# Scores and skip of one more batch as plain fp32 products, in a cross-attention and feed-forward kernel on one core

## The chip, the core and the metric

The kernel runs on one core of a Trainium2 chip. Its time is the device time of one execution in microseconds (us); lower is better. A core has five engines with a queue each: TensorE (PE in the profile; its weight loads are PEld), VectorE (DVE), ScalarE (ACT), GpSimd (POOL) and the sync engine (SP), which here only starts transfers. Each engine works off its own instructions in order; semaphores tie the queues together.

## What is computed

For each of 32 batches, x is 128 rows of 1024 and ctx is 128 rows of 256:

```
xl = layernorm(x)                                  # over the 1024
q = Wq xl;  k = Wk ctx;  v = Wv ctx                # 128 channels
att = softmax(q^T k / sqrt(128))                   # 1024 x 256
x1 = x + Wskip xl + v att^T
out = x1 + layernorm(x1) @ dequant(qweight, scales, zeros) + bias    # 1024 x 1024
```

The weights of the last product are four-bit numbers, unpacked once. The products are wanted nearly in fp32 precision.

## The kernel before

Wq is folded into the keys, so the scores are a product of the centred rows of x (128 x 1024) with scaled keys (128 x 256): eight tiles of 128 x 256 for each batch, in four chunks of two tiles. The two tiles of a chunk lie in ps_e[j % 2], so chunk j can only be written when the exps of chunk j - 2 (of the batch before, for j below 2) have been read.

There are two ways to form scores and skip. Batches from WHOLE (4) on are *split*: centred rows, keys and skip weights are each held as a high part in fp32r and a low part (the difference), and a product is three fp32r matmuls, high-high, high-low and low-high (`HI_LO`, L974 for the scores, L1009 for the skip). Batches 0 to 3 are *whole*: centred rows, keys and skip weights stay in plain fp32 (x_whole, k_whole, wsk_whole, with one slot for each of the four) and a product is one fp32 matmul instruction of the program, which the trace records as two passes (L970, L1005). The low parts cost VectorE and GpSimd work, the high part of the rows a copy on ScalarE.

The work is a software pipeline. Each engine has a hand-written run_in for the first batches and a step(t) for t = 3 on; in step t the engines work on scores and softmax of batch b = t, on projections of batch n = t + 1, on the attention product, skip and second norm of a = t - 1, and on the feed-forward product of q = t - 2. What an engine does in a step, and in which order, stands in that list. The parts that matter here:
- TensorE, step (L1105): scores(b, 0), keys_values(n) (L978), skip(a, 0) (L1000) and attend(a, 0) (L1011), scores(b, 1), scores(b, 2), skip(a, 1), attend(a, 1), scores(b, 3), then 34 feed-forward matmuls (L1020, L1026).
- ScalarE, step (L582): centre(n) (L456), exps(b, 0) (L499), keys_hi(n) (L469), values_hi(n) (L481), centred_hi(n) (L463), exps(b, 1), exps(b, 2), probs_hi(b, 0) (L510, the fp16 high part of the probabilities, L515), exps(b, 3), context_hi, apply_norm2(a) (L519), probs_hi(b, 1), xn_high(a).
- VectorE, step (L869): a row maximum (L695) ahead of each exps and a reciprocal (L700, called invert) behind it, keys_lo(n) (L681) and values_lo(n) (L687) in the middle, residual(a, h) (L711), the statistics of the norms, aggregate2(a) (L725) with the variance (L731), probs_lo (L704), scale_product (L734), context_lo (L659).
- GpSimd, step (L413): normalise(b, 0) (L270), inverse_std1, centred_lo(n, 0) (L284), normalise(b, 1), normalise(b, 2), centred_lo(n, 1), inverse_std2(a) (L291, with the bias of the second norm in L297), normalise(b, 3), write_out(q, 0) (L262, the add into o_sb in L267), split_row_sum(a), xn_low(a), write_out of the other half.
- The sync engine loads x and ctx, turns the probabilities and the normed rows by DMA and stores the output.

The projected keys are split too, from batch 5 on (SPLIT_KEYS); context_lo at t = 3 makes the low part of batch 5's context for keys_values(5) (L988), which step 4 of TensorE needs. In the rows, a line such as L974 is a line of the kernel.

Of the kernel before, what the change touches and what calls it, by code (L numbers as in the profile page):

```python
# [11 lines left out]
ACT = mybir.ActivationFunctionType  # L12
# [3 lines left out]
def xattn_ffn_program(nc, x, ctx_in, wq, wk, wv, wskip, qweight, scales, zeros, bias, out):  # L16


    B, C, N = x.shape
    M = ctx_in.shape[2]  # L20
# [2 lines left out]
    HALF = 512  # L23
    SPLIT_KEYS = 5
    QUARTER = 256
    WHOLE = 4
    HALVES = N // HALF
    NT = N // P
    MT = M // P
# [16 lines left out]
    with es:  # L46
        def sb(name, shape, dt=F32):
            return es.enter_context(nc.sbuf_tensor("sb_" + name, shape, dt))
# [37 lines left out]
        k_hi, k_lo = (sb(n, [P, 2, M], F32R) for n in ("k_hi", "k_lo"))  # L86
        v_hi, v_lo = (sb(n, [P, 3, M], F16) for n in ("v_hi", "v_lo"))
        wsk_hi, wsk_lo = (sb(n, [C, 3, C], F32R) for n in ("wsk_hi", "wsk_lo"))
        x_whole, k_whole, wsk_whole = (sb(n, [P, WHOLE, k]) for n, k in (("x_whole", N), ("k_whole", M), ("wsk_whole", C)))
        prob = sb("prob", [P, 2, CHUNKS, TPC, M])  # L90
        neg_max = sb("neg_max", [P, CHUNKS, TPC])
        esum = sb("esum", [P, CHUNKS, TPC])
# [46 lines left out]
        def ran(b, back=0):  # L139
            return 0 <= b - back < B  # L140
# [106 lines left out]
        def _(pool):  # L247
# [165 lines left out]
            def step(t):  # L413
                m, n, b, a, q, c = t + 2, t + 1, t, t - 1, t - 2, t - 3
                if 0 <= c < B - 1:
                    write_out(c, 1)
                if ran(b):
                    normalise(b, 0)
                if ran(m):
                    inverse_std1(m)  # L420
                if ran(n):
                    centred_lo(n, 0)
                if ran(b):
                    normalise(b, 1)
                    normalise(b, 2)
                if ran(n):
                    centred_lo(n, 1)
                if ran(a):
                    inverse_std2(a)
                if ran(b):  # L430
                    normalise(b, 3)
                if ran(q) and a < B - 1:
                    write_out(q, 0)
                if ran(a):
                    split_row_sum(a)
                    xn_low(a)
                if ran(q) and a >= B - 1:
                    write_out(q, 0)
# [5 lines left out]
        def _(act):  # L444
# [11 lines left out]
            def centre(n):  # L456
                act.wait_ge(mv1_done, n + 1)
                if n > WHOLE:
                    act.wait_ge(xclo_done, HALVES * (n - WHOLE))
                act.activation(xc[:, :] if n >= WHOLE else x_whole[:, n, :], x_sb[:, n % 4, :],  # L460
                               ACT.Identity, bias=mv1[:, 0:1], scale=-1.0).then_inc(xc_done, 1)

            def centred_hi(n):  # L463
# [5 lines left out]
            def keys_hi(n):  # L469
                if n < 2:  # L470
                    act.wait_ge((k0_done, k1_done)[n], 1)
                else:
                    act.wait_ge(kv_done, n + 1)
                act.wait_ge(rstd1_done, n + 1)
                if ran(n, WHOLE + 2):
                    act.wait_ge(scores_done[3], n - 1)
                src = (ps_o[1], ps_y[0], ps_kv)[min(n, 2)]
                act.activation(k_hi[:, n % 2, :] if n >= WHOLE else k_whole[:, n, :], src[:, 0:M], ACT.Copy,
                               scale=rstd1[:, n % 2:n % 2 + 1]).then_inc(khi_done, 1)

            def values_hi(n):  # L481
                act.wait_ge(t_step, 4 * (n + 1))
                act.wait_ge(kv_done, n + 1)
                if ran(n, 3):
                    act.wait_ge(attn_done[1], n - 2)
                act.activation(wsk_hi[:, n % 3, :] if n >= WHOLE else wsk_whole[:, n, :], proj[:, SKIP, :], ACT.Copy, scale=sk_scale[:, :])
                act.activation(v_hi[:, n % 3, :], ps_kv[:, M:2 * M], ACT.Copy,
                               scale=v_scale[:, :]).then_inc(kvhi_done, 1)

# [92 lines left out]
            def step(t):  # L582
                n, b, a = t + 1, t, t - 1
                if ran(n):
                    centre(n)
                if ran(b):
                    exps(b, 0)
                if ran(n):
                    keys_hi(n)
                    values_hi(n)  # L590
                    centred_hi(n)
                if ran(b):
                    exps(b, 1)
                if ran(b):
                    exps(b, 2)
                    probs_hi(b, 0)
                if ran(b):
                    exps(b, 3)
                if ran(t + 2) and t >= 3:
                    if t == 3:  # L600
                        key_projection_hi()
                    context_hi(t + 2)
                if ran(a):
                    apply_norm2(a)
                if ran(b):
                    probs_hi(b, 1)
                if ran(a):
                    xn_high(a)
# [5 lines left out]
        def _(dve):  # L614
# [254 lines left out]
            def step(t):  # L869
                m, n, b, a, q, c = t + 2, t + 1, t, t - 1, t - 2, t - 3  # L870
                if ran(c) and c < B - 1:
                    scale_product(c, 1)
                if c == B - 1:
                    last_out(0)
                    last_out(1)
                if ran(b):
                    row_max(b, 0)
                if ran(n):
                    value_scale(n)
                if ran(m):  # L880
                    stats1(m, 0)
                    stats1(m, 1)
                    aggregate1(m)
                if ran(b):
                    invert(b, 0)
                if ran(m):
                    variance1(m)
                if ran(a):
                    residual(a, 0)
                if ran(b):  # L890
                    row_max(b, 1)
                    row_max(b, 2)
                if ran(a):
                    stats2(a, 0)
                if ran(b):
                    invert(b, 1)
                if ran(n):
                    keys_lo(n)
                    values_lo(n)
                if ran(b):  # L900
                    invert(b, 2)
                if ran(a):
                    residual(a, 1)
                if ran(b):
                    row_max(b, 3)
                if ran(a):
                    stats2(a, 1)
                    aggregate2(a)
                if ran(b):
                    invert(b, 3)  # L910
                    probs_lo(b, 0)
                if ran(m):
                    context_max(m)
                if ran(q):
                    scale_product(q, 0)
                if ran(m) and t >= 3:
                    if t == 3:
                        key_projection_lo()
                    context_lo(m)
                if a == B - 1:  # L920
                    last_low()
                if ran(b):
                    probs_lo(b, 1)
# [5 lines left out]
        def _(pe):  # L929
# [23 lines left out]
            def scores(b, j):  # L953
                if b < WHOLE:
                    if j == 0:
                        pe.wait_ge(xc_done, b + 1)
                        pe.wait_ge(khi_done, b + 1)
                else:
                    if j == 0:
                        pe.wait_ge(klo_done, b - WHOLE + 1)  # L960
                    if j % (CHUNKS // HALVES) == 0:
                        pe.wait_ge(xclo_done, HALVES * (b - WHOLE) + 1 + j // (CHUNKS // HALVES))
                if j >= 2:
                    pe.wait_ge(exp_done[j - 2], b + 1)
                elif ran(b, 1):
                    pe.wait_ge(exp_done[j + 2], b)
                for t in range(TPC):
                    cols = slice((j * TPC + t) * P, (j * TPC + t + 1) * P)
                    if b < WHOLE:
                        last = pe.matmul(ps_e[j % 2][:, t, :], x_whole[:, b, cols],  # L970
                                         k_whole[:, b, :], start=True, stop=True)
                        continue
                    for i, (s, m) in enumerate(HI_LO):
                        last = pe.matmul(ps_e[j % 2][:, t, :], xc_p[s][:, b % 3, cols], k_p[m][:, b % 2, :],  # L974
                                         start=i == 0, stop=i == 2)
                last.then_inc(scores_done[j], 1)
# [23 lines left out]
            def skip(a, h):  # L1000
# [1 line left out]
                if ran(a, 1):  # L1002
                    pe.wait_ge(x1_done[h], a)
                if a < WHOLE:
                    pe.matmul(ps_o[h][:, :], wsk_whole[:, a, :], x_whole[:, a, cols],  # L1005
                              start=True, stop=False)
                    return
                for i, (s, m) in enumerate(HI_LO):
# [145 lines left out]
```

## Time and profile before

| | |
|---|---|
| median of 3 runs | 517.02 us (516.99 to 517.34) |
| the profiled execution's own time | 517.71 us |
| its span in the trace | 515.6 us |
| TensorE busy | 496.5 us (96%) |
| GpSimd busy | 467.1 us (91%) |
| VectorE busy | 435.3 us (84%) |
| ScalarE busy | 376.8 us (73%) |
| share of the chain of work that ended last, TensorE | 83% |
| the same, GpSimd | 8% |

Times in the trace count from the start of the span. The ends of matmuls are modelled and neighbours overlap: for the pace of TensorE one reads the distance between the starts, not the durations. The chain that ended last is followed back from the last instruction, at each step to what released it. "[x <-y]" at the end of a timeline row is idle time ahead of the instruction and who ended it. A share of the whole span says little about one step, so the prediction goes by steps.

### The profile page before, as it was taken

The page shows a single profiled execution, that of the slowest core. Times are in us where ns is not written, and L with a number is a line of the kernel's source. Part 1 is how long each engine was busy: PE and PEld are TensorE (multiplying, and loading weights), DVE is VectorE, ACT ScalarE, POOL GpSimd, SP SyncE. Part 2 cuts the span into 40 slices and gives each one's busy share as a digit, 9 for nine tenths or more (in the row PEclk, how much of TensorE's full clock was granted, in tenths as well). Part 3 has the DMA queues.
Part 4 walks back from the last instruction along what each step waited for, and adds up shares of the span by engine and source line. Part 5 has one row for each costly group of instructions (what it writes and reads, how often), then busy time and mean ns, then how long its engine had stood idle before and what let it go on. Part 6 is the DMA issues. An engine that isn't in the chain of part 4 may idle for free.

```text
span 515.6 us, 9359 instructions
## 1 busy us (share of the span) xinstructions
PE 496.5 (96%) x2672; PEld 299.4 (58%) x2672; DVE 435.3 (84%) x1001; ACT 376.8 (73%) x867; POOL 467.1 (91%) x711
## 2 busy tenths in 40 slices
PE   4888999999999999999999999999999999999987
PEld 3544456665666656566665566666556666565644
DVE  4989898888988888898888889888889888887752
ACT  4889778777787777778777777877777877777520
POOL 4786999999999999999999999999999999999763
PEclk9999999999999999999999999999999999999999
DMA  8774678778968987887878786787767687757653
GB/s 305 204 156 108 183 176 157 204 187 187 197 171 202 156 199 183 196 182 179 211 150 193 185 206 176 180 204 156 196 178 197 172 202 190 168 130 145 167 130 120
DMA packets 227203, 92.65 MB, mean 180 GB/s; under 512 B 209488, under 2 KB 214352, under 8 KB 227152
## 3 DMA queue, kind: packets, MB, share of 16 engines
q1 hardware_dynamic: 226432, 91.91, 73.9%
q8 instruction: 21, 0.34, 0.3%
q14 instruction: 30, 0.25, 0.2%
q10 hardware_dynamic: 720, 0.14, 0.2%
HBM read 23.87 MB, written 16.78 MB: 79 GB/s over the span
## 4 chain that ended last, share of the span: by engine, by line
PE 83%; POOL 8%; issue 3%; DVE 3%; ACT 2%; DMA 1%; POOLq 0%; ACTq 0%; SPq 0%
PE ps_y L1020 38%; PE ps_e L974 15%; PE ps_o L1015 13%; PE ps_o L1009 7%; PE ps_kv L992 2%; PE ps_y L1026 2%; PE ps_kv L988 2%; POOL sb_prob L273 2%; POOL sb_xn_lo L318 2%; PE ps_e L970 1%; POOL sb_o L267 1%; DMA sb_x<-in_x_dram 1%; ACT sb_prob L506 1%; POOL sb_rstd L281 1%; DVE sb_neg_max L697 1%
## 5 line engine op out<-in xcount | busy, mean ns | idle before, releaser
L1020 PE MATMUL ps_y<-sb_wf,sb_xnt_hi 128*128 128x512 f16 x496 | 188.3, 380 | 3.3 <-DMA sb_xnt_lo<-sb_xn_lo 3.3
L1020 PE MATMUL ps_y<-sb_wf,sb_xnt_lo 128*128 128x512 f16 x496 | 188.0, 379 | 0.0
L506 ACT ACTIVATE sb_prob<-ps_e,sb_neg_max 128x256 f32<-128x256 f32 x256 | 118.2, 470 | 51.5 <-DVE sb_neg_max L697 51.4
L273 POOL TENSOR_SCALAR sb_prob<-sb_prob,sb_rsum 128x256 f32<-128x256 f32 x256 | 122.5, 492 | 7.3 <-DVE sb_rsum L702 7.2
L706 DVE TENSOR_TENSOR sb_p_lo<-sb_prob,sb_p_hi 128x1024 f16<-128x1024 f32 x64 | 78.1, 1220 | 36.5 <-ACT sb_p_hi L515 36.4
L267 POOL TENSOR_TENSOR sb_o<-sb_prod,sb_x 128x512 f32<-128x512 f32 x63 | 84.9, 1348 | 5.8 <-DVE sb_prod L740 5.8
L697 DVE TENSOR_REDUCE sb_neg_max<-ps_e 128x2 f32<-128x512 f32 x128 | 85.0, 682 | 1.8 <-PE ps_e L970 1.4
L515 ACT ACTIVATE sb_p_hi<-sb_prob 128x1024 f16<-128x1024 f32 x64 | 67.4, 1053 | 23.3 <-issue 23.3
L1020 PEld LDWEIGHTS ps_y<-sb_wf,sb_xnt_hi 128*128 128x128 f16 x496 | 48.4, 98 | 61.0 <-DMA sb_xnt_lo<-sb_xn_lo 4.3
L1020 PEld LDWEIGHTS ps_y<-sb_wf,sb_xnt_lo 128*128 128x128 f16 x496 | 48.5, 98 | 54.8
L974 PE MATMUL ps_e<-sb_k_hi,sb_xc_hi 128*128 128x256 f32 x224 | 78.6, 351 | 0.1
L524 ACT ACTIVATE sb_xn<-sb_x,sb_nb,sb_rstd 128x1024 f32<-128x1024 f32 x32 | 43.3, 1353 | 42.4 <-POOL sb_nb L297 42.4
L318 POOL TENSOR_TENSOR sb_xn_lo<-sb_xn,sb_xn_hi 128x512 f16<-128x512 f32 x63 | 71.8, 1161 | 0.2
L288 POOL TENSOR_TENSOR sb_xc_lo<-sb_xc,sb_xc_hi 128x512 fp32r<-128x512 f32 x56 | 71.2, 1272 | 0.0
L974 PE MATMUL ps_e<-sb_k_lo,sb_xc_hi 128*128 128x256 f32 x224 | 63.1, 281 | 0.0
L974 PE MATMUL ps_e<-sb_k_hi,sb_xc_lo 128*128 128x256 f32 x224 | 62.8, 280 | 0.0
L740 DVE TENSOR_TENSOR sb_prod<-ps_y,sb_scale_row 128x512 f32<-128x512 f32 x63 | 42.9, 682 | 11.2 <-PE ps_y L1026 6.3
L506 ACT ACTIVATION_READ_ACCUMULATOR sb_prob<-ps_e,sb_neg_max 128x1 f32 x256 | 51.1, 199 | 0.0
L716 DVE SCALAR_TENSOR_TENSOR sb_x<-ps_o,sb_o_scale,sb_x 128x512 f32<-128x512 f32 x64 | 47.3, 739 | 2.9 <-PE ps_o L1015 2.8
L1015 PE MATMUL ps_o<-sb_pt_hi,sb_v_hi 128*128 128x512 f16 x128 | 49.1, 384 | 0.4 <-DMA sb_pt_lo<-sb_p_lo 0.4
L1015 PE MATMUL ps_o<-sb_pt_hi,sb_v_lo 128*128 128x512 f16 x128 | 48.5, 379 | 0.0
L1015 PE MATMUL ps_o<-sb_pt_lo,sb_v_hi 128*128 128x512 f16 x128 | 48.5, 379 | 0.0
(150 smaller groups left out, 976.0 us busy)
## 6 DMA issues: line engine op xcount, KB each, us to landing
sb_x<-in_x_dram SPq DMA_DIRECT2D x32, 512.0 KB, 3.9
out_dram<-sb_o SPq DMA_DIRECT2D x63, 256.0 KB, 2.4
sb_ctx<-in_ctx_dram SPq DMA_DIRECT2D x32, 128.0 KB, 2.7
sb_q<-in_L_ffn_qweight_dram SPq DMA_DIRECT2D x4, 512.0 KB, 7.5
sb_pt_hi<-sb_p_hi SPq DMA_TRANSPOSE x64, 3.0
sb_pt_lo<-sb_p_lo SPq DMA_TRANSPOSE x64, 2.9
sb_scale_row<-in_L_ffn_scales_dram SPq DMA_DIRECT2D x1, 512.0 KB, 9.6
sb_xnt_hi<-sb_xn_hi SPq DMA_TRANSPOSE x32, 2.8
```

What stands on the lines that cost most here:

```text
L267: pool.tensor_tensor(o_sb[:, c % 2, cols], prod[:, h, :], x1[:, c % 3, cols], ALU.add).then_inc(out_done[h], 1)
L273: last = pool.tensor_scalar(prob[:, b % 2, j, t, :], prob[:, b % 2, j, t, :], rsum[:, j, t:t + 1], P_SCALE, ALU.mult, ALU.mult)
L288: pool.tensor_tensor(xc_lo[:, n % 3, cols], xc[:, cols], xc_hi[:, n % 3, cols].bitcast(F32), ALU.subtract).then_inc(xclo_done, 1)
L318: last = pool.tensor_tensor(xn_lo[:, k:k + KT // 2, :], xn[:, k:k + KT // 2, :], xn_hi[:, k:k + KT // 2, :], ALU.subtract)
L506: done = act.activation(prob[:, b % 2, j, t, :], ps_e[j % 2][:, t, :], ACT.Exp, bias=neg_max[:, j, t:t + 1], accum_out=esum[:, j, t:t + 1])
L515: act.activation(p_hi[:, h, :, :].rearrange("n k (t m) -> n k t m", m=P), prob[:, b % 2, 2 * h:2 * h + 2, :, :].rearrange("n j t (k m) -> ...
L697: dve.tensor_reduce(neg_max[:, j, :], ps_e[j % 2][:, :, :], AX.X, ALU.max, negate=True).then_inc(max_done[j], 1)
L706: dve.tensor_tensor(p_lo[:, h, :, :].rearrange("n k (t m) -> n k t m", m=P), prob[:, b % 2, 2 * h:2 * h + 2, :, :].rearrange("n j t (k m) ...
L716: dve.scalar_tensor_tensor(x1[:, a % 3, cols], ps_o[h][:, :], o_scale[:, a % 3:a % 3 + 1], x_sb[:, a % 4, cols], ALU.mult, ALU.add).then_i ...
L974: last = pe.matmul(ps_e[j % 2][:, t, :], xc_p[s][:, b % 3, cols], k_p[m][:, b % 2, :], start=i == 0, stop=i == 2)
L1015: last = pe.matmul(ps_o[h][:, :], v_p[s][:, a % 3, k * P:(k + 1) * P], pt_p[m][:, h, k, :], start=False, stop=k == MT - 1 and i == 2)
L1020: pe.matmul(ps_y[h][:, :], xnt_p[s][:, q % 2, kt, :], wf[:, kt, h * HALF:(h + 1) * HALF], start=kt == 0 and s == 0, stop=False)
```

## The change

Batch 4 becomes a whole batch. WHOLE is 5, while the three fp32 tiles keep their four slots (SLOTS); batch 4 uses slot 0, which was batch 0's. ScalarE gets two waits ahead of writing it: centre(4) waits for batch 0's attention product (behind its skip), keys_hi(4) for batch 0's last scores. For batch 4 centred_hi, centred_lo (two halves), keys_lo and the low part of the skip weights (in values_lo) are left out; scores (eight tiles) and skip (two halves) are one fp32 matmul each in place of three fp32r ones. SPLIT_KEYS stays at 5.

```diff
-    WHOLE = 4
+    WHOLE, SLOTS = 5, 4
...
-        x_whole, k_whole, wsk_whole = (sb(n, [P, WHOLE, k]) for n, k in (("x_whole", N), ("k_whole", M), ("wsk_whole", C)))
+        x_whole, k_whole, wsk_whole = (sb(n, [P, SLOTS, k]) for n, k in (("x_whole", N), ("k_whole", M), ("wsk_whole", C)))
...
-                if ran(n):
+                if ran(n) and n >= WHOLE:
                     centred_lo(n, 0)
...
-                if ran(n):
+                if ran(n) and n >= WHOLE:
                     centred_lo(n, 1)
...
                 if n > WHOLE:
                     act.wait_ge(xclo_done, HALVES * (n - WHOLE))
-                act.activation(xc[:, :] if n >= WHOLE else x_whole[:, n, :], x_sb[:, n % 4, :],
+                if SLOTS <= n < WHOLE:
+                    act.wait_ge(attn_done[1], n - SLOTS + 1)
+                act.activation(xc[:, :] if n >= WHOLE else x_whole[:, n % SLOTS, :], x_sb[:, n % 4, :],
                                ACT.Identity, bias=mv1[:, 0:1], scale=-1.0).then_inc(xc_done, 1)
...
                 if ran(n, WHOLE + 2):
                     act.wait_ge(scores_done[3], n - 1)
+                elif SLOTS <= n < WHOLE:
+                    act.wait_ge(scores_done[3], n - SLOTS + 1)
                 src = (ps_o[1], ps_y[0], ps_kv)[min(n, 2)]
-                act.activation(k_hi[:, n % 2, :] if n >= WHOLE else k_whole[:, n, :], src[:, 0:M], ACT.Copy,
+                act.activation(k_hi[:, n % 2, :] if n >= WHOLE else k_whole[:, n % SLOTS, :], src[:, 0:M], ACT.Copy,
                                scale=rstd1[:, n % 2:n % 2 + 1]).then_inc(khi_done, 1)
...
-                act.activation(wsk_hi[:, n % 3, :] if n >= WHOLE else wsk_whole[:, n, :], proj[:, SKIP, :], ACT.Copy, scale=sk_scale[:, :])
+                act.activation(wsk_hi[:, n % 3, :] if n >= WHOLE else wsk_whole[:, n % SLOTS, :], proj[:, SKIP, :], ACT.Copy, scale=sk_scale[:, :])
...
                     keys_hi(n)
                     values_hi(n)
+                if ran(n) and n >= WHOLE:
                     centred_hi(n)
...
                 if ran(n):
-                    keys_lo(n)
+                    if n >= WHOLE:
+                        keys_lo(n)
                     values_lo(n)
...
                     if b < WHOLE:
-                        last = pe.matmul(ps_e[j % 2][:, t, :], x_whole[:, b, cols],
-                                         k_whole[:, b, :], start=True, stop=True)
+                        last = pe.matmul(ps_e[j % 2][:, t, :], x_whole[:, b % SLOTS, cols],
+                                         k_whole[:, b % SLOTS, :], start=True, stop=True)
                         continue
...
                 if a < WHOLE:
-                    pe.matmul(ps_o[h][:, :], wsk_whole[:, a, :], x_whole[:, a, cols],
+                    pe.matmul(ps_o[h][:, :], wsk_whole[:, a % SLOTS, :], x_whole[:, a % SLOTS, cols],
                               start=True, stop=False)
                     return
```

## Rows read from the trace of the kernel before

**Rows 1.** Chain of waits in order of time: start us, us, what; "x" counts instructions.
```profile
75.11 0.31 POOL sb_xc_lo L288
...
480.33 0.75 DVE sb_x L716
```
**Rows 2.** Windows of step 4 and step 5: busy us and count of each engine, granted clock.
```profile
67.40:83.44 16.04, 15.82 (x85) 9.01 (x83) 14.45 (x33) 12.73 (x30) 15.64 (x24) 1.00 0.77 185
83.44:98.58 15.14, 15.14 (x87) 9.27 (x85) 13.55 (x32) 11.84 (x28) 14.82 (x22) 1.00 0.82 186
```
**Rows 3.** Timeline of TensorE, steps 4 and 5: start us, busy us, line, tiles.
```profile
68.28 0.18 PE L983 MATMUL ps_m<-sb_amax,sb_ones 128*128 128x1 bf16 x1
68.57 0.36 PE L988 MATMUL ps_kv<-sb_ctx_lo,sb_key_hi 128*128 128x256 f32 x1
...
74.97 0.38 PE L1015 MATMUL ps_o<-sb_pt_hi,sb_v_lo 128*128 128x512 f16 x1
75.46 0.39 PE L974 MATMUL ps_e<-sb_k_hi,sb_xc_hi 128*128 128x256 f32 x1
...
76.28 0.39 PE L1020 MATMUL ps_y<-sb_wf,sb_xnt_hi 128*128 128x512 f16 x1
...
84.33 0.18 PE L983 MATMUL ps_m<-sb_amax,sb_ones 128*128 128x1 bf16 x1
84.37 0.36 PE L988 MATMUL ps_kv<-sb_ctx_lo,sb_key_hi 128*128 128x256 f32 x1
```
**Rows 4.** Timeline of ScalarE, steps 3 and 4.
```profile
56.61 1.07 ACT L467 ACTIVATE sb_xc_hi<-sb_xc 128x1024 fp32r<-128x1024 f32 x1
58.19 0.47 ACT L506 ACTIVATE sb_prob<-ps_e,sb_neg_max 128x256 f32<-128x256 f32 x1 [0.52 <-DVE sb_neg_max L697]
...
59.91 0.21 ACT L506 ACTIVATION_READ_ACCUMULATOR sb_prob<-ps_e,sb_neg_max 128x1 f32 x1
62.54 1.06 ACT L515 ACTIVATE sb_p_hi<-sb_prob 128x1024 f16<-128x1024 f32 x1 [2.41 <-issue]
...
75.20 0.20 ACT L506 ACTIVATION_READ_ACCUMULATOR sb_prob<-ps_e,sb_neg_max 128x1 f32 x1
```
**Rows 5.** Timeline of TensorE, step 3: plain fp32 scores and skip of whole batches.
```profile
49.76 1.03 PE L970 MATMUL ps_e<-sb_k_whole,sb_x_whole 128*128 128x256 f32 x4
50.62 0.17 PE L983 MATMUL ps_m<-sb_amax,sb_ones 128*128 128x1 bf16 x1
...
51.61 1.02 PE L1005 MATMUL ps_o<-sb_x_whole,sb_wsk_whole 128*128 128x512 f32 x2
```
**Rows 6.** Chain of waits: split scores and a split skip where TensorE never waits.
```profile
87.43 1.43 PE ps_e L974 x12
...
452.32 0.69 PE ps_o L1009 x3
```
**Rows 7.** Timeline of GpSimd, step 3.
```profile
60.28 1.27 POOL L288 TENSOR_TENSOR sb_xc_lo<-sb_xc,sb_xc_hi 128x512 fp32r<-128x512 f32 x1
...
65.20 0.75 POOL L297 TENSOR_SCALAR sb_nb<-sb_mv,sb_rstd 128x1 f32<-128x1 f32 x1
...
66.83 1.30 POOL L267 TENSOR_TENSOR sb_o<-sb_prod,sb_x 128x512 f32<-128x512 f32 x1
```
**Rows 8.** Timeline of VectorE, steps 3 and 4.
```profile
59.34 0.47 DVE L684 SCALAR_TENSOR_TENSOR sb_k_lo<-ps_kv,sb_rstd,sb_k_hi 128x256 fp32r<-128x256 f32 x1
...
60.40 0.15 DVE L702 RECIPROCAL sb_rsum<-sb_esum 128x2 f32<-128x2 f32 x1
...
62.68 0.15 DVE L731 TENSOR_SCALAR sb_ve<-sb_mv 128x1 f32<-128x1 f32 x1
...
66.92 1.51 DVE L661 TENSOR_TENSOR sb_ctx_lo<-sb_ctx,sb_ctx_hi 128x256 fp32r<-128x256 f32 x1
...
73.67 1.28 DVE L697 TENSOR_REDUCE sb_neg_max<-ps_e 128x2 f32<-128x512 f32 x2
...
81.53 0.46 DVE L661 TENSOR_TENSOR sb_ctx_lo<-sb_ctx,sb_ctx_hi 128x256 fp32r<-128x256 f32 x1
```

## The prediction, made before the changed kernel ran

> **What bounds the kernel now.** The page's busy times come first: TensorE is the busiest engine, GpSimd the next. Then the chain of waits in order of time. Up to 75.42 us its pieces in steps 3 and 4 are GpSimd's; then come the last scores of batch 4, and from there it stays on TensorE up to 480.33 us, where the tail of the last batches begins [rows 1]. The windows say how firmly: step 5, from 83.44 to 98.58 us, holds 15.14 us of TensorE work in 15.14 us, and the 25 steps behind it are as long; step 4 holds 15.82 us in 16.04 [rows 2]. So an instruction that TensorE gains in step 5 or later moves the end by its whole length, while step 4 has holes that can take some in. What matters for GpSimd's place in the chain is how long TensorE itself stood still. Its timeline shows two holes. From L983 to L988 it needs 68.57 - 68.28 = 0.29 us where step 5 needs 0.04: 0.25 us lost. The last scores of batch 4 start at 75.46 us, while the attention matmul that started at 74.97 has left the array free after its usual 0.215 us of issue, at 75.18: 0.28 us lost. Behind that stop the chunk needs 0.82 us, up to the first L1020 at 76.28, where an undisturbed one needs half of 1.43, 0.71: another 0.11 us [rows 3, 6]. Step 4 can give back 0.25 + 0.28 + 0.11 = **0.64 us** at most. The holes of step 3 are out of reach: the first instruction that goes, the copy to xc_hi, starts at 56.61 us, and ScalarE waits behind it for VectorE's row maximum until 58.19 anyway [rows 4], so the exps that TensorE waits for in step 3 end when they do now.
>
> **What TensorE gets.** Each score chunk of two tiles becomes four passes of plain fp32 instead of six of fp32r. Fewer instructions, yet the distance between issues decides. A plain chunk takes 50.62 - 49.76 = 0.86 us, and its last result comes 0.17 us after that (1.03 us in all) [rows 5]. Two split chunks take 1.43 us [rows 6]. Four chunks: 4 x 0.86 = 3.44 against 2 x 1.43 = 2.86, **+0.58 us**, all in step 4. The skip goes from three passes of 512 columns, 0.69 us [rows 6], to two, which stream as much as a chunk's four of 256 and show 1.02 us with the same 0.17 of drain, 0.85 [rows 5]: +0.16 for each half, **+0.32 us**, in step 5, where nothing absorbs it. Together +0.90 us.
>
> A rule speaks against this price. The Trainium skill, FP8 and Floating Point Precision, section TensorE Precision Notes, says that true fp32 takes four passes through the array. Counted against the three of the split, by that rule both terms would be a third of the old time, (2.86 + 1.38) / 3 = 1.41 us, as an estimate. The trace puts a plain tile at 0.43 us, not at 4/3 of 0.36 = 0.48, so I stay with the rows.
>
> **What the other engines lose.** ScalarE drops 1.07 us into an idle stretch (above): nothing by itself. GpSimd drops both halves of xc_lo, 1.27 us each [rows 7]. VectorE drops k_lo, 0.47 us, and wsk_lo behind it [rows 8]. What then comes earlier, followed through the queues:
> - VectorE's next reciprocal, at 60.40 us [rows 8], needs ScalarE's exps, which end at 59.91 + 0.21 = 60.12 [rows 4]. Only some 0.26 us of what was dropped is a lead; the variance for the second norm, at 62.68 to 62.83 [rows 8], ends near 62.57.
> - GpSimd starts normalise(3,1) near 60.3, in the place of L288 at 60.28 [rows 7]. ScalarE's p_hi, at 62.54 now because it needs that normalise, starts 1.3 us earlier [rows 4], and so do the exps behind it. The bias of the second norm, 65.20 now [rows 7], needs only the reciprocal square root before it, 0.64 us behind the variance: near 63.24, 1.96 earlier.
> - VectorE works without a pause from the reciprocal behind those exps on, so their 1.3 us carries. Context_lo of batch 5, 66.92 + 1.51 = 68.43 us now, ends near 67.1 [rows 8]. It is what TensorE waits for in the first hole: it comes there at 68.28 now and at 68.43 behind the longer scores [rows 3]. Closed, with 1.3 us to spare.
> - TensorE comes to the last scores of batch 4 at 75.18 + 3/4 of 0.58 - 0.25 = 75.37 us. The maxima that release them start at 73.67 now [rows 8] and could start at 72.4, but need scores(4,1). Those leave TensorE before a chunk, a skip half and an attention half (6 x 0.215): 75.37 - 0.86 - 0.85 - 1.29 = 72.37, and 0.17 later they are there, 72.54. The exps behind the maxima, which end at 75.20 + 0.20 = 75.40 now [rows 4], then end near 74.3. Closed, with 1.1 us to spare.
>
> Behind step 4 the three engines are ahead, TensorE is not. The sync engine's queue keeps its transfers, with those of p_hi, p_lo and xn earlier. The two new waits on ScalarE (centre for batch 0's attention, keys_hi for its scores) are on counts reached long before 52 us; the exps are queued behind them. They cost nothing as long as ScalarE's idle stretch covers them, some hundredths without it.
>
> **Sum.** +0.58 + 0.32 - 0.64 = **+0.26 us**. The profiled execution took 517.71 us, its span 515.6; the change would put it at 517.97. It stands 0.69 above the median of the runs, 517.02, to which the same difference applies: 517.3 us. The unknown is how much of the 0.64 comes back: none gives +0.90, all +0.26, and I take all, since both leads are above 1 us.
>
> **The rivals.** A measurement of this kernel can tell about 0.2%, 1.03 us, from no change.
> - *The holes stay, or move.* Context_lo took 1.51 us for its usual 0.46 [rows 8] beside GpSimd's 1.30 us add into o_sb [rows 7]; a stretch of that kind can fall on another VectorE instruction now. Against: it takes over 1.1 us on a queue that is 1.3 ahead. Price: +0.90, 517.9 us. The Trainium skill, SBUF — State Buffer, section Who interferes with whom, says that a VectorE instruction with two SBUF inputs and a GpSimd one that reads SBUF exclude each other, and that issue order decides; the trace agrees, with that 1.51.
> - *Slower beyond that.* Two such stretches, 2 x 1.05 us, between VectorE's maxima of scores(4,0) and scores(4,1) use up the slack of 1.1 and put 1.0 us in front of the last scores. The point from which it decides is 1.1 us of delay there; then +0.26 + 1.0 = 1.26, 518.3 us. Against: step 4 has one such stretch now, before those maxima.
> - *A plain pass costs a third more than the split.* If scores and skips cost four passes of split length among their split neighbours, +1.41 - 0.64 = +0.77, 517.8 us. Against: plain skips stand in step 4 already, between split scores. It is what the rule of four passes makes of the time.
> - *Faster: GpSimd paces this stage, as the chain says.* Then 75.46 comes 1.3 us earlier and carries all behind it: -1.3 + 0.15 (the last plain chunk) + 0.32 = -0.8, 516.2 us; with all 2.5 us of GpSimd's -2.0, 515.0 us. Against: TensorE has 0.64 us of holes to lose there, not more.
> - *The tail uses a lead kept from step 4.* Against: the 26 steps between are paced by TensorE, so a lead is spent in waiting.
> That the change doesn't do what it says I leave out: slot 0 of the three tiles is free by then, and writer and readers index it alike.
>
> **Chances.** Forecast 0.70; holes stay 0.11; four passes 0.05; slower beyond 0.05; faster 0.05, about half of it inside 0.2%; something no row shows 0.04. So faster by over 0.2% 0.04, within 0.2% 0.87, slower by over 0.2% 0.09. The range reaches below the forecast by about the scatter of the runs, 0.35 us, and a little of the faster case, above through the holes that stay: 516.8 to 518.1 us.
>
> **What would show it.** On TensorE: 16 plain passes for batch 4's scores, 0.215 us apart; L988 0.04 us behind L983; no idle time ahead of the last scores; the first L1020 behind them within 0.1 us of 76.28; skips of batch 4 at 0.85; steps of 15.14 us behind. On GpSimd: normalise(3,1) near 60.3, then idle time ahead of its next add into o_sb. On VectorE: context_lo ending near 67.1. I am wrong if idle time stands ahead of a TensorE group of step 4 (first two rivals), or if batch 5's scores start well ahead of now (GpSimd's).

## The result: slower by half a per cent, most of it in the tail

The changed kernel takes 519.53 us (median of 6 runs, 519.02 to 521.11), the kernel before 517.03 (6 runs, 516.92 to 517.34): a ratio of 1.0051, 95% interval 1.0040 to 1.0061. That is slower, and outside the predicted range of 516.8 to 518.1 us. The profiled execution took 519.8 us, its span is 517.7.

The first look goes to the steps that the change touches. The timeline of the changed kernel, steps 3 to 5 (start us, busy us, engine, line, tiles; in this kernel L976 is the plain scores, L989 and L994 are what L983 and L988 were, L1021 what L1015 was, L1026 what L1020 was; L519 writes p_hi, L702 the row maxima):

```profile
60.19 1.83 POOL L273 TENSOR_SCALAR sb_prob<-sb_prob,sb_rsum 128x256 f32<-128x256 f32 x4
61.20 1.06 ACT L519 ACTIVATE sb_p_hi<-sb_prob 128x1024 f16<-128x1024 f32 x1 [1.17 <-issue]
63.24 1.30 POOL L297 TENSOR_SCALAR sb_nb<-sb_mv,sb_rstd 128x1 f32<-128x1 f32 x1
65.54 1.52 DVE L666 TENSOR_TENSOR sb_ctx_lo<-sb_ctx,sb_ctx_hi 128x256 fp32r<-128x256 f32 x1
...
68.33 0.17 PE L989 MATMUL ps_m<-sb_amax,sb_ones 128*128 128x1 bf16 x1
68.36 0.36 PE L994 MATMUL ps_kv<-sb_ctx_lo,sb_key_hi 128*128 128x256 f32 x1
...
72.46 0.69 DVE L702 TENSOR_REDUCE sb_neg_max<-ps_e 128x2 f32<-128x512 f32 x1
73.33 0.69 DVE L702 TENSOR_REDUCE sb_neg_max<-ps_e 128x2 f32<-128x512 f32 x1 [0.17 <-PE ps_e L976]
...
75.06 0.38 PE L1021 MATMUL ps_o<-sb_pt_hi,sb_v_lo 128*128 128x512 f16 x1
75.28 1.03 PE L976 MATMUL ps_e<-sb_k_whole,sb_x_whole 128*128 128x256 f32 x4
76.14 0.38 PE L1026 MATMUL ps_y<-sb_wf,sb_xnt_hi 128*128 128x512 f16 x1
...
84.19 0.18 PE L989 MATMUL ps_m<-sb_amax,sb_ones 128*128 128x1 bf16 x1
```

Both holes of [rows 3] are closed: L994 follows L989 by 0.03 us (0.29 before), and the last scores of batch 4 start 0.22 us behind the attention matmul ahead of them, with no idle time named. The chunk costs 76.14 - 75.28 = 0.86 us, as a plain chunk does in [rows 5]. Context_lo ends at 67.06, where 67.1 was forecast (it took 1.52 us again, as before, and the lead covers that); the bias of the second norm, p_hi and normalise(3,1) stand about 0.1 us from their forecasts or nearer. The chain of waits, which had GpSimd's xc_lo at 75.11 us [rows 1], is TensorE's alone from 59.86 us on, through both steps.

The windows of steps 4 and 5 say the same. Windows of the changed kernel (busy us and count of PE, PEld, DVE, ACT, POOL; then granted clock, DMA share, GB/s):

```profile
67.43:83.29 15.86, 15.81 (x74) 8.98 (x75) 14.20 (x32) 12.36 (x29) 15.07 (x22) 1.00 0.72 177
83.29:98.75 15.46, 15.41 (x84) 9.06 (x83) 13.48 (x32) 11.68 (x28) 14.46 (x22) 1.00 0.88 182
```

To see where the time went, one instruction is followed from batch to batch: the matmul with the column of ones (L983 before, L989 after), which stands once in each batch's keys. Its starts, from the timelines of TensorE, and the end of the span:

| stretch, us | before | after | difference |
|---|---|---|---|
| start of the span to batch 4 | 50.62 | 50.52 | -0.10 |
| batch 4 to 6 (scores, holes) | 33.71 | 33.67 | -0.04 |
| batch 6 to 7 (skip of batch 4) | 15.14 | 15.46 | +0.32 |
| batch 7 to 31 | 363.46 | 363.41 | -0.05 |
| batch 31 to the end of the span | 52.70 | 54.67 | **+1.97** |

So the change cost 0.28 us where it was made, and 2 us more than 380 us later. The table adds up to 2.10 us, by which the two profiled executions differ (2.09); the medians lie 2.50 apart. For the other 0.4 us there are the starts of single executions, which scatter by more than that, and a lower clock in two of the six runs (under e2).

There the chain of waits names the place; it is the same chain in both kernels up to the last transfer. First the kernel before, then the one after (start us, us, what):

```profile
494.28 2.84 DMA sb_xnt_lo<-sb_xn_lo
497.12 0.05 issue
497.16 2.98 PE ps_y L1020 x13
```

```profile
494.36 4.87 DMA sb_xnt_lo<-sb_xn_lo
499.23 0.05 issue
499.28 2.76 PE ps_y L1026 x12
```

The transfer that turns the low part of the normed rows of batch 30 starts 0.08 us later and takes 2.03 us more. TensorE has nothing else left to do. Its idle time in the grouped lines of 494 to 502 us (line, operation, tiles, count, busy us and mean ns, idle before and who ended it), before and after:

```profile
L1020 PE MATMUL ps_y<-sb_wf,sb_xnt_hi 128*128 128x512 f16 x11 | 4.2, 380 | 1.4 <-DMA sb_xnt_lo<-sb_xn_lo 1.4
```

```profile
L1026 PE MATMUL ps_y<-sb_wf,sb_xnt_hi 128*128 128x512 f16 x7 | 2.7, 381 | 3.4 <-DMA sb_xnt_lo<-sb_xn_lo 3.4
```

Windows of one microsecond show a stop and not a slow transfer (columns as above). Before, then after:

```profile
495.00:496.00 1.00, 0.80 (x4) 0.19 (x2) 0.47 (x2) 0.00 (x0) 0.44 (x1) 1.00 0.65 148
496.00:497.00 1.00, 0.00 (x0) 0.00 (x0) 0.97 (x2) 0.00 (x0) 0.00 (x0) 1.00 0.98 248
497.00:498.00 1.00, 0.84 (x4) 0.41 (x5) 0.68 (x3) 0.00 (x0) 0.17 (x1) 1.00 1.07 412
```

```profile
495.00:496.00 1.00, 0.88 (x5) 0.20 (x2) 0.47 (x2) 0.00 (x0) 0.51 (x1) 1.00 0.71 148
496.00:497.00 1.00, 0.00 (x0) 0.00 (x0) 0.97 (x2) 0.00 (x0) 0.00 (x0) 1.00 2.43 23
497.00:498.00 1.00, 0.00 (x0) 0.00 (x0) 0.76 (x3) 0.00 (x0) 0.09 (x1) 1.00 0.06 6
```

From 496 to 498 us the DMA engines move 23 and 6 GB/s, where they moved 248 and 412. A packet is put down whole to the time at which it began, which is how the share comes above 1: these packets are in flight and don't end. The DMA view of 490 to 500 us says what is new. Queues and the two transfers behind which the others wait, before and after (queue, kind: packets, MB, share; then transfer, KB, us to landing):

```profile
q14 instruction: 1, 0.01, 0.3%
...
out_dram<-sb_o SPq DMA_DIRECT2D x2, 256.0 KB, 2.3
...
sb_xnt_lo<-sb_xn_lo SPq DMA_TRANSPOSE x1, 2.8
```

```profile
q8 instruction: 1, 0.02, 1.2%
...
out_dram<-sb_o SPq DMA_DIRECT2D x2, 256.0 KB, 3.5
...
sb_xnt_lo<-sb_xn_lo SPq DMA_TRANSPOSE x1, 4.9
```

Queue q8 fetches instructions, 16,384 bytes at a time, 21 times in either run. Its single packets, and the slow ones of the transposes, as the trace has them (queue, start us, ns, bytes):

```
before   q8   489.75   992  16384
after    q8   495.48  1900  16384
after    q1   496.01  2134    256      18 such packets, 496.01 to 496.15,
after    q1   496.15  2005    256      2005 to 2138 ns; their neighbours take 18
```

The fetch, which stood ahead of the transposes of the normed rows, stands on the one of xn_lo, and 18 of that transfer's packets, begun while it runs, take 2.1 us for their usual 18 ns. Such packets are no feature of the tail: in all eleven traces together 730 packets of 256 bytes took over 1.5 us, and 719 of them were in flight during a fetch on q8. The kernel before has 20 of them (131.21 to 131.35 us, 1.86 to 2.00 us), where TensorE waits for nothing.

Why the fetch moved is a count. 21 fetches of 256 instructions hold 5,376, and TensorE issues about that: 5,502 before, of which 2,672 are matmuls, as many weight loads, the rest nearly all waits. The change takes ten matmul passes, ten weight loads and one wait from its queue: 21 instructions. (The page's counts of weight loads are 2,672 before and 2,662 after; of the matmuls after, 32 records are missing.) That leads to theory A: **the position of TensorE's last instruction fetch, not batch 4, costs the 2 us**.

### The profile page after: what moved, and what is told of

Read it like the earlier page. It is cut to its first block, busy times and chain, and to the rows that moved or that the text cites. A ratio compares the mean times of both kernels' runs of the same rounds, so it can differ in the third digit from the quotient of the medians.

```text
span 517.7 us, 9299 instructions
## 1 busy us (share of the span) xinstructions
PE 495.2 (96%) x2630; PEld 299.0 (58%) x2662; DVE 434.7 (84%) x999; ACT 376.4 (73%) x866; POOL 465.0 (90%) x709
## 4 chain that ended last, share of the span: by engine, by line
PE 85%; POOL 5%; DVE 3%; issue 3%; DMA 2%; ACT 2%; POOLq 0%; ACTq 0%; SPq 0%
PE ps_y L1026 40%; PE ps_e L980 14%; PE ps_o L1021 14%; PE ps_o L1015 7%; PE ps_kv L994 2%; PE ps_kv L998 2%; PE ps_e L976 2%; POOL sb_prob L273 1%; PE ps_y L1032 1%; POOL sb_xn_lo L318 1%; DMA sb_xnt_lo<-sb_xn_lo 1%; DMA sb_x<-in_x_dram 1%; DVE sb_neg_max L702 1%; ACT sb_prob L510 1%; PE ps_o L1011 1%
## 5 line engine op out<-in xcount | busy, mean ns | idle before, releaser
L1026 PE MATMUL ps_y<-sb_wf,sb_xnt_hi 128*128 128x512 f16 x496 | 188.3, 380 | 6.8 <-DMA sb_xnt_lo<-sb_xn_lo 5.2
L1026 PE MATMUL ps_y<-sb_wf,sb_xnt_lo 128*128 128x512 f16 x496 | 188.0, 379 | 0.0
L702 DVE TENSOR_REDUCE sb_neg_max<-ps_e 128x2 f32<-128x512 f32 x128 | 85.2, 683 | 1.8 <-PE ps_e L976 1.4
L1026 PEld LDWEIGHTS ps_y<-sb_wf,sb_xnt_hi 128*128 128x128 f16 x496 | 48.4, 98 | 62.8 <-DMA sb_xnt_lo<-sb_xn_lo 6.2
L519 ACT ACTIVATE sb_p_hi<-sb_prob 128x1024 f16<-128x1024 f32 x64 | 67.3, 1052 | 20.6 <-issue 20.6
L1026 PEld LDWEIGHTS ps_y<-sb_wf,sb_xnt_lo 128*128 128x128 f16 x496 | 48.5, 98 | 54.9
L980 PE MATMUL ps_e<-sb_k_hi,sb_xc_hi 128*128 128x256 f32 x216 | 75.9, 351 | 0.0
L288 POOL TENSOR_TENSOR sb_xc_lo<-sb_xc,sb_xc_hi 128x512 fp32r<-128x512 f32 x54 | 68.7, 1272 | 0.0
L980 PE MATMUL ps_e<-sb_k_lo,sb_xc_hi 128*128 128x256 f32 x216 | 60.8, 281 | 0.0
L980 PE MATMUL ps_e<-sb_k_hi,sb_xc_lo 128*128 128x256 f32 x216 | 60.6, 281 | 0.0
L1021 PE MATMUL ps_o<-sb_pt_hi,sb_v_hi 128*128 128x512 f16 x128 | 49.1, 384 | 0.4 <-DMA sb_pt_lo<-sb_p_lo 0.4
L1021 PE MATMUL ps_o<-sb_pt_hi,sb_v_lo 128*128 128x512 f16 x128 | 48.5, 379 | 0.0
L1021 PE MATMUL ps_o<-sb_pt_lo,sb_v_hi 128*128 128x512 f16 x128 | 48.5, 379 | 0.0
```

Source lines behind the costliest of these rows:

```text
L288: pool.tensor_tensor(xc_lo[:, n % 3, cols], xc[:, cols], xc_hi[:, n % 3, cols].bitcast(F32), ALU.subtract).then_inc(xclo_done, 1)
L519: act.activation(p_hi[:, h, :, :].rearrange("n k (t m) -> n k t m", m=P), prob[:, b % 2, 2 * h:2 * h + 2, :, :].rearrange("n j t (k m) -> ...
L702: dve.tensor_reduce(neg_max[:, j, :], ps_e[j % 2][:, :, :], AX.X, ALU.max, negate=True).then_inc(max_done[j], 1)
L1021: last = pe.matmul(ps_o[h][:, :], v_p[s][:, a % 3, k * P:(k + 1) * P], pt_p[m][:, h, k, :], start=False, stop=k == MT - 1 and i == 2)
L1026: pe.matmul(ps_y[h][:, :], xnt_p[s][:, q % 2, kt, :], wf[:, kt, h * HALF:(h + 1) * HALF], start=kt == 0 and s == 0, stop=False)
```

## The experiments

Where a kernel below is said to carry waits, they are waits on counts reached long before, one instruction for two of them.

**e1_after_pad21: give back the count.** The changed kernel with the 21 instructions put back at the start of TensorE's queue, where it waits for the first loads in any case.

```diff
+            for k in range(42):
+                pe.wait_ge((ident_zero, ident_made)[k % 2], 1)
             pe.wait_ge(wkq_loaded, 32)
```

> The changed kernel with 42 semaphore waits at the very start of TensorE's queue, where it waits over 5 us for its first weights anyway; they are met at once, and become 21 instructions, as many as the change takes out of TensorE's queue. Theory A (the extra 2 us is a fetch of TensorE's instructions, 16 KB every 256 instructions, that the change moved from 489.75 us to 495.48 us, onto the transposes of xn_lo for batch 30 in the tail): the fetch goes back to about 490 us, that transfer lands after 2.8 us again instead of 4.9, and the time is 517.0 + 0.3 = 517.3 us. Theory B (the tail is longer because GpSimd, VectorE or the transfers reach it in another order after the change): the added waits change nothing there, 519.5 us. Theory C (the difference lies in TensorE's own work of steps 4 and 5): 519.5 us as well, with the time lost before 100 us.

Measured: 517.31 us (10 runs, 517.00 to 517.97) against 517.04 of the kernel before on the same chip, 1.0007 (0.9997 to 1.0016). The last fetch is at 489.74 us, and from batch 31 on it takes 52.76 us (52.70 before, 54.67 after). The DMA view of 490 to 500 us and the grouped lines are those of before again:

```profile
q14 instruction: 1, 0.01, 0.2%
...
sb_xnt_lo<-sb_xn_lo SPq DMA_TRANSPOSE x1, 2.8
```

```profile
L1028 PE MATMUL ps_y<-sb_wf,sb_xnt_hi 128*128 128x512 f16 x11 | 4.2, 380 | 1.4 <-DMA sb_xnt_lo<-sb_xn_lo 1.4
```

The whole change is in this kernel, and the 2 us are gone; theories B and C had 519.5 us. That what is left of the medians, +0.27 us, is so near the prediction's +0.26 is in part luck, since the interval goes from -0.2 to +0.8 us; the trace has +0.29 from batch 4 to 7.

**e2_after_pad21_end: the same waits at the other end.** As e1, but with the waits ahead of the last feed-forward product, behind all that fetches: the control for the waits themselves.

```diff
                 if q == B - 1:
+                    for k in range(42):
+                        pe.wait_ge((ident_zero, ident_made)[k % 2], 1)
                     last_ffn()
```

> The control: the same 42 waits (21 instructions), placed just ahead of the last feed-forward product, behind the fetch at 495 us in the queue. Theory A: the fetch stays near 495.5 us and the transfer lands after about 4.9 us: 519.5 us (plus up to 0.5 us for the waits themselves). If added waits as such, or another layout of the program, cured the tail: 517.3 us.

Measured: 521.12 us (4 runs, 519.07 to 521.25), 1.0067 (1.0045 to 1.0088); fetch at 495.22, landing 4.8 us, TensorE waits 3.3. It is not the length of the program that counts, but how many instructions stand ahead of the tail. The waits themselves cost nothing here: they are worked off from 504.07 to 506.32 us, while the matmuls in front of them still run, up to 507.93 us. That e2 is even slower than the changed kernel is a second effect. The windows of e2 behind TensorE's wait:

```profile
499.00:500.00 1.00, 1.00 (x3) 0.31 (x3) 0.00 (x0) 0.99 (x2) 0.00 (x0) 0.51 0.60 231
500.00:501.00 1.00, 1.00 (x4) 0.38 (x3) 0.00 (x0) 0.98 (x1) 0.71 (x4) 0.50 0.02 8
501.00:502.00 1.00, 1.00 (x4) 0.38 (x3) 0.00 (x0) 0.08 (x1) 0.88 (x2) 0.50 0.00 0
502.00:503.00 1.00, 1.00 (x5) 0.38 (x4) 0.00 (x0) 0.00 (x0) 0.31 (x1) 0.79 0.82 189
```

The granted clock is at the lower of its two levels, 1.2 GHz, for some 3.4 us behind the wait, and the grouped line of the same stretch has matmuls of 634 ns for 379:

```profile
L1026 PE MATMUL ps_y<-sb_wf,sb_xnt_lo 128*128 128x512 f16 x4 | 2.5, 634 | 0.0
```

From batch 31 on e2 takes 56.26 us, 1.6 more than the changed kernel's profiled run, whose clock stayed at 2.4 GHz. The price can be read more sharply, from the end of TensorE's wait to the end of the span: 18.46 us before, 18.46 after and 18.47 in e3, where the clock stays up; 20.14 in e2, 20.13 in e4 and 20.14 in e8, where it goes down: 1.7 us. The runs of the changed kernel itself fall in two groups: 520.31 and 521.11 us with a mean clock of 0.997, the others, 519.02 to 519.80, with 1.0. So do e2's, 521.08 to 521.25 and one of 519.07. Behind the 1.4 us wait of the kernel before, the clock of its profiled run stays up, and no run of it in the experiments has a mean clock below 0.999.

**e3_before_less20: the effect without the change.** The kernel before, with ten attention matmuls (20 instructions) left out: the two low-part products of batch 0 and a part of batch 1's. Nothing of the change is in it.

```diff
+                        if i and (a == 0 or i == a == 1 and h == 0):
+                            continue
...
```

> The other way round: the kernel before, with 10 matmul instructions (20 instructions of the queue with their weight loads) left out of the attention product of batches 0 and 1, where TensorE waits for other engines anyway. Left out are the terms with a low part of batch 0 and, of batch 1, the term with the low part of the probabilities in the first half. Theory A: TensorE's fetch near 490 us moves to about 495 us, onto the transposes of xn_lo, and the kernel before becomes slower by some 2 us though it does less: about 519 us. Theories B and C: 517.0 us or a little less (at most 2.2 us less).

Measured: 520.41 us (4 runs, 519.86 to 520.76), 1.0065 (1.0050 to 1.0080), though it computes less; theories B and C had 517.0 us or less. Its DMA view of 490 to 500 us, and its grouped line of 494 to 503:

```profile
q8 instruction: 1, 0.02, 0.8%
...
sb_xnt_lo<-sb_xn_lo SPq DMA_TRANSPOSE x1, 4.7
```

```profile
L1022 PE MATMUL ps_y<-sb_wf,sb_xnt_hi 128*128 128x512 f16 x8 | 3.0, 380 | 3.2 <-DMA sb_xnt_lo<-sb_xn_lo 3.2
```

From batch 31 on it takes 54.50 us, 1.80 more than the kernel before; its clock stayed up, while the other three runs have a mean clock of 0.997. The other microsecond of its profiled run lies at the start, where its first keys come 1.15 us later: VectorE waits 1.05 us for the load of Wskip, and not at all before. The starts of these kernels scatter: the matmul with the ones of batch 4 comes at 49.66 to 52.10 us, e8 left aside.

**e4_after_pad10: half the count.** As e1, with 20 waits (10 instructions).

```diff
+            for k in range(20):
+                pe.wait_ge((ident_zero, ident_made)[k % 2], 1)
             pe.wait_ge(wkq_loaded, 32)
```

> The changed kernel with half the padding: 20 waits, 10 instructions, at the start. Theory A: the fetch falls between the two places, at some 492 to 493 us, while the probabilities and xn_hi are turned and before xn_lo is; if it ends before 494.3 us the time is 517.3 us, if it still meets the transfers of xn_hi, in front of xn_lo in the same queue, up to 519.5 us. Theories B and C: 519.5 us.

Measured: 520.12 us (4 runs, 518.34 to 520.34), 1.0052 (1.0035 to 1.0070). The fetch did not move to 492 or 493 us: it came at 494.57, 32.41 us behind batch 31's matmul, where it is in the changed kernel (32.42). The transpose, issued at 493.46, took 4.5 us:

```profile
q8 instruction: 1, 0.02, 1.0%
...
sb_xnt_lo<-sb_xn_lo SPq DMA_TRANSPOSE x1, 4.5
```

Three of its four runs have the lower clock (0.997) as well; the fourth, with 1.0, took 518.34 us. The direction holds (not enough instructions, and the 2 us stay), the size of the step was wrong: the fetch doesn't move in proportion to the count.

**e5_scores_alone and e6_skip_alone: the parts.** Two constants, SC for the scores and SK for the skip, in place of WHOLE; the part that stays split keeps its high and low halves. Each carries the waits that make up for what it drops from TensorE's queue (17 and 4 instructions).

```diff
-                if b < WHOLE:
+                if b < SC:
...
-                if a < WHOLE:
+                if a < SK:
```

> Only the scores of batch 4 are plain fp32; its skip stays split, so the copy to xc_hi and both halves of xc_lo stay too, and only keys_lo goes. 17 instructions of padding at the start of TensorE's queue keep its fetches where the kernel before has them. Theory of the sum: TensorE gains 0.58 us in step 4, but the two holes there close because TensorE itself arrives later, with GpSimd as late as before (0.15 of 0.25 us at context_lo and a lead of VectorE from keys_lo for the rest, 0.28 + 0.11 us ahead of the last scores): between 0.0 and +0.15 us, 517.1 us. Rival (the holes closed in the full change because GpSimd lost 2.5 us): the holes stay open here and the time is up to 517.6 us.

> Only the skip of batch 4 is plain; its scores stay split, with xc_hi, xc_lo and keys_lo; the low part of the skip weights goes. 4 instructions of padding. Theory of the sum: +0.32 us of TensorE work in step 5 where nothing absorbs it, and the holes of step 4 stay within 0.1 us of what they are: 517.3 us. Rival: the skip's price is hidden by waits of step 5, 517.0 us.

Measured, scores alone: 517.43 us (10 runs) against 517.25, 1.0005 (0.9995 to 1.0014); batch 4 to 6 takes 33.93 us, +0.22, and nothing changes behind it. Skip alone: 517.44 us (10 runs), 1.0010 (1.0000 to 1.0019); batch 4 to 6 33.74, batch 6 to 7 15.45: +0.34. The skip is as forecast, the scores are just above. With GpSimd's xc_lo still made, the first hole is only half closed, as the timeline of e5 has it:

```profile
68.21 0.17 PE L993 MATMUL ps_m<-sb_amax,sb_ones 128*128 128x1 bf16 x1
68.37 0.36 PE L998 MATMUL ps_kv<-sb_ctx_lo,sb_key_hi 128*128 128x256 f32 x1
```

L998 stands 0.16 us behind L993 (0.29 before, 0.03 after). At the last scores 0.14 us stays too: they start at 75.31 us, 0.25 behind the attention matmul ahead of them (0.22 after), and need 0.97 us up to the first L1030 (0.86 after). The parts add up to 0.56, the whole to 0.28: the low part of the rows can only be left out when both are made.

**e7_before_nolo4: the low part of the rows.** The kernel before, with GpSimd's two halves of xc_lo for batch 4 left out; scores and skip of batch 4 read the high part in their place, as many matmuls as before.

```diff
-                if ran(n):
+                if ran(n) and n > WHOLE:
                     centred_lo(n, 0)
```

> The kernel before without GpSimd's two instructions for the low part of batch 4's centred rows; TensorE runs the same products with the high part in its place, so its queue has the same instructions. Left out: the low part of batch 4's rows in scores and skip. Theory of the sum: TensorE's holes in step 4, 0.64 us, are all there is to win: 516.4 us. Rival (GpSimd paces the stage, as the chain of waits has it): 2.5 us or at least 1.3 us less, 514.5 to 515.7 us.

Measured: 516.65 us (10 runs) against 517.25, 0.9993 (0.9983 to 1.0002). Batch 4 to 6 takes 33.11 us, -0.60. (The times of e5, e6 and e7 alone can hardly be told from no change, so their readings rest on the starts in the traces.) Scores and skip leave out the low part of batch 4's rows here. That is what GpSimd's place in the chain is worth: the holes of TensorE, 0.64 at most by the prediction, and not GpSimd's 1.3 or 2.5 us. The terms measured one by one are then +0.58 (all of 4 x 0.86 - 2.86, since the chunk measures 0.86), +0.31 and -0.60, 0.29 in sum; the whole change measures 0.28.

**e8_before_pad235: once round.** If blocks of 256 count, 235 more instructions ahead of the kernel before leave the fetch where 21 fewer do, only one fetch later: 470 waits, at the place of e1's.

> The kernel before, nothing left out, with 470 waits (235 instructions) ahead of TensorE's first matmul: 235 + 21 = 256, so TensorE's fetches stand to its instructions as in the changed kernel. Theory A: a fetch again meets the transposes of xn_lo of batch 30 and that transfer lands after some 4.9 us instead of 2.8, +2 us between the last split scores and the end, on top of whatever the waits delay the start by (0 if all 235 pass within the 5.4 us that TensorE waits for its weights, 2 to 10 us if not). If the fetch is not what matters: 2.8 us for that transfer, and the same distance from step 5 to the end as in the kernel before.

Measured: 541.08 us (2 runs). Most of that is the waits themselves: they start 0.11 us apart (106 ns in the median), the last at 26.5 us, and TensorE's first matmul comes at 26.64 us for 5.44, 21 us later, where at most 10 were expected. So the time says nothing here; the tail does. There are 22 fetches, the last one 32.48 us behind batch 31's matmul (32.42 after, 26.83 before), and the DMA view of 510 to 520 us shows it on the transpose:

```profile
q8 instruction: 1, 0.02, 1.2%
...
sb_xnt_lo<-sb_xn_lo SPq DMA_TRANSPOSE x1, 4.7
```

TensorE waits 3.5 us there, the clock goes down behind it, and from batch 31 on it takes 56.43 us, as in e2. Taking 21 away and putting 235 in do the same, as a period of 256 has it. The counts fit: from one fetch to the next TensorE starts 255 instructions here on average, and 253 to 257 in the others. (The changed kernel, with its missing records, is left out.)

**e9_after_pad36: neither the old count nor the new one.** As e1, with 72 waits (36 instructions).

> The changed kernel with 72 met waits (36 instructions) at the start of TensorE's queue, so neither the count of the kernel before nor that of the change: 15 instructions more than before. Theory A (what counts is where TensorE's last instruction fetch falls, not that the old count is restored): 15 instructions are about 3 us of matmuls, so the last fetch comes some 3 us before that of the kernel before, near 486.5 to 487.5 us, at least 3 us ahead of the transposes of xn_hi; landing of xn_lo 2.8 us, TensorE waits 1.4 us, 517.3 us (ratio 1.0007), as long as the waits at 0.1 us each (3.6 us) are covered by the wait for the first loads. Rival (only the old phase is good, or the waits themselves help): 519 us or more, landing near 4.8. If the waits are not covered, the start is up to 1 us later and the tail as before.

Measured: 517.57 us (10 runs, 517.05 to 519.74) against 517.42, 1.0006 (0.9996 to 1.0016). Its profiled run started 0.9 us late and is 2.1 behind at batch 31, so places are told from batch 31's matmul: the last fetch is 24.81 us behind it, 2.0 before that of the kernel before (3 expected), and the rest of the run takes 52.70 us, exactly that of before. So 15 instructions more than before are as good as the old count. What matters is where the fetch falls. By chance this run also shows one in the middle that is not quite hidden. Its chain of waits holds

```profile
330.88 4.90 DMA sb_xnt_lo<-sb_xn_lo
```

with a fetch of TensorE's at 332.19 us (1.74 us long), and the step in which it lies, from 328.34 to 343.88 by the matmul with the ones, took 15.54 us for 15.14. There a transfer that lands 2 us late costs 0.4. The profiled run of e7 has the same: a fetch at 420.27 us, the transfer of xn_lo from 418.46 us taking 4.95, and a step of 15.50 us.

## Why the prediction was wrong

Point by point, by its own steps:
- *What bounds steps 4 and 5*: right. TensorE paces them, GpSimd is in the chain of [rows 1] only through the 0.64 us of holes. e7 gave back 0.60 of it.
- *What TensorE gets*: right to 0.01 us, a chunk 0.86 and the skip +0.32. The rival of a pass that costs a third more, which the rule of four passes would make of it, would have put +0.77 there; the trace has +0.28. The rule's count isn't refuted by that, only the price: a plain tile's 0.43 us is about four times the 0.109 us of an fp16 matmul of 256 columns (0.87 us for eight in the tail of before), while the three of the split cost 0.119 each (1.43 us for twelve [rows 6]).
- *What the other engines lose*: right in every place that was named, to about 0.1 us. Only the first feed-forward matmul behind the scores was to stand within 0.1 us of 76.28 and stands at 76.14; 0.10 of that is the earlier start.
- *The sum*: +0.26 us; +0.28 in the trace from batch 4 to batch 7, +0.27 in e1. As the price of the edit where it is made it was right; as a forecast of the time it lacked a term.
- *"Behind step 4 the three engines are ahead, TensorE is not. The sync engine's queue keeps its transfers"*: **this is the step that failed**, and with it the dismissal of the fifth rival, that the tail can change only through a lead kept from step 4. Each engine's work was followed through its queue, and so was each transfer that the kernel issues. The instructions themselves are transfers too. That TensorE issues 21 fewer never entered the sum as a count, though the profile before lists queue q8 with 21 packets. The missing term is the tail, and it measured +1.97 us; where the clock falls as well, 1.7 more. The signs of being wrong that the prediction named all stand in steps 4 and 5, so none of them would have shown it.
- *The chances*: slower by over 0.2% had 0.09, of it 0.05 through stretches in step 4 that did not come and 0.04 for something that no row shows. That last is what came.

The Trainium skill, Runtime: NRT & Kernel Launch, section Instruction fetch mechanics, says that a queue is refilled in blocks of 16 KiB, 256 instructions, over a DMA queue of its own, and that crossing a block is mostly hidden. The trace agrees with the blocks for TensorE (packets of 16,384 bytes; 21 and 22 fetches), not for queue q14, whose packets have 8,192 bytes. Hidden it is as well, between batch 7 and 31, which take 363.4 us in both kernels, though the fetches lie elsewhere; the 0.4 us of e9 and e7 are the most that was seen there. It is not hidden in the tail, where TensorE waits for the one transfer on which the fetch falls.

What stays open: why that transfer's packets stand still for 2.1 us while the fetch runs (e1 to e9 show when, not how; that the fetch is the cause, and not only there at the same time, rests on the counts: it is there in five kernels and not in six, and the traces show no other difference between them in front of that transfer's landing); what sets the fetch off, since it jumped by 5.6 us between e4's count and the kernel before's, 11 instructions apart, and didn't move between e4's and the changed kernel's (counted from the end of TensorE's work it comes 172 to 174 instructions ahead in the five kernels, e2's waits left aside, and 223 to 245 in the six, so it isn't bound to a fixed instruction); and why the clock falls behind a wait of 3.1 to 3.5 us in some executions and not in others.

## What to carry to other kernels

When a change takes instructions from an engine or adds some, count them: from there on, each of its instruction fetches falls elsewhere, and a fetch that meets a DMA transpose on which the engine waits cost 2 us here, against 0.3 us of what the change itself did. A small difference is put down to an edit only when it stands at the edit; a table of one instruction's starts, batch by batch, shows that in five rows. To measure such an edit by itself, make up the count with waits that are already met, where the engine waits anyway and for as many as fit there (0.11 us for each instruction).

## What the runs showed of the hardware

- A fetch of TensorE's instructions (queue q8, 16,384 bytes) took 0.9 to 1.9 us. When it fell on the DMA transpose of the tail, that transfer landed after 4.5 to 4.9 us for 2.8 in all five kernels where this was so, and the 256 KB stores behind it took 3.3 to 3.5 us for 2.3. In the other six it landed after 2.8 to 2.9 us.
- A fetch on another queue (q14, 8,192 bytes, at 499.5 us in the kernel before) took 0.53 us, at a time without a transpose.
- A met wait is no free instruction: 235 instructions of waits started 0.11 us apart in TensorE's queue and put its first matmul off by 21.2 us (e8). The 21 of e2, behind which no matmul was due yet, cost nothing.
- Behind a wait of 3.1 to 3.5 us, TensorE's granted clock went down to 1.2 GHz for some 3.4 us in e2, e4 and e8, and not in the profiled runs of the changed kernel and of e3 (waits of 3.4 and 3.2 us). It cost 1.7 us: 20.13 to 20.14 us from the end of that wait to the end of the span, for 18.46 to 18.47.
